# Spreading the gates of two expert pairs at once from two copies of the gate rows

## The reference

```python
# 1: linear attention over 8 heads of 8 channels, on layer-normed channels
k = relu(conv1x1(x, Wk, bk)); q = relu(conv1x1(x, Wq, bq)); v = conv1x1(x, Wv, bv)
context = einsum('bhkn,bhvn->bhkv', k, v)          # over all 16384 positions
x = x + conv1x1(einsum('bhkv,bhkn->bhvn', context, q), Wr, br)
# 2: mixture of 8 experts per position, on layer-normed tokens t
probs = softmax(t @ router_w + router_b); top_p, top_i = top_k(probs, 2)
top_p = top_p / sum(top_p)
expert_out = einsum('bnd,edc->bnec', t, expert_w) + expert_b
t = t + sum over the two chosen experts of top_p * expert_out
```

## Time and profile before

| what | value |
|---|---|
| median of 3 runs | 672.26 us (671.27 to 673.7) |
| the profiled execution | 671.9 us, its span 670.1 us |
| granted TensorE clock, mean | 0.992 |
| PE busy | 616.2 us, 92% |
| DVE, ACT, POOL busy | 515.1 (77%), 425.2 (63%), 396.1 us (59%) |
| spread matmuls, L1078 | 1024, busy 93.2 us |
| expert matmuls, L1092 and L1095 | 512 each, side by side, 243.6 us |
| DMA, mean | 129 GB/s |

### The profile page before, as it was taken

One profiled execution on the slowest core, in us unless ns is written; L12 is line 12 of the kernel. 1 busy time (PEld: TensorE's weight loads), 2 busy tenths in 40 slices (PEclk: granted clock), 3 DMA queues, 4 the chain that ended last, 5 costly groups with the idle time before them and its releaser, 6 DMA issues.

```text
span 670.1 us, 21498 instructions
## 1 busy us (share of the span) xinstructions
PE 616.2 (92%) x8318; PEld 276.3 (41%) x8318; DVE 515.1 (77%) x1176; ACT 425.2 (63%) x832; POOL 396.1 (59%) x350
## 2 busy tenths in 40 slices
PE   3799989779999999999999999999999999998887
PEld 1566656444444444444444444444332332332222
DVE  3534455978888888889788787987799999989844
ACT  2355545576666675766757576766766776766642
POOL 7232342237565655666666556655577777777875
PEclk9799989999999999999999999999999999999999
DMA  6223635666555566655545665554565667446542
GB/s 149 56 76 79 146 97 129 150 167 159 122 122 134 126 147 146 159 142 138 133 111 130 147 152 127 129 116 104 133 154 127 157 172 170 101 111 142 126 111 48
DMA packets 32662, 86.21 MB, mean 129 GB/s; under 512 B 7650, under 2 KB 7826, under 8 KB 32562
## 3 DMA queue, kind: packets, MB, share of 16 engines
q1 hardware_dynamic: 32082, 84.64, 52.8%
q0 software_dynamic: 288, 0.19, 0.2%
q10 hardware_dynamic: 192, 0.01, 0.0%
HBM read 34.47 MB, written 16.78 MB: 76 GB/s over the span
## 4 chain that ended last, share of the span: by engine, by line
PE 62%; DVE 18%; ACT 10%; issue 7%; DMA 1%; POOL 1%; ACTq 0%; DVEq 0%; SPq 0%; POOLq 0%
PE bank L1092 26%; PE bank L1078 7%; PE bank L1015 5%; PE bank L993 4%; PE bank L979 4%; DVE z L826 3%; PE bank L938 3%; PE bank L1089 3%; PE bank L962 3%; DVE x L731 3%; ACT grows L569 2%; DVE xnT L686 2%; PE bank L1039 2%; DVE osb L836 2%; ACT L529 2%
## 5 line engine op out<-in xcount | busy, mean ns | idle before, releaser
L442 POOL TENSOR_TENSOR z<-gbs,x1d 128x512 f32<-128x512 f32 x256 | 320.2, 1275 | 185.2 <-ACT gbs L575 72.6
L1095 PE MATMUL bank<-z,ew 128*64 128x512 f32 x512 | 243.7, 598 | 0.0
L1092 PE MATMUL bank<-z,ew 128*64 128x512 f32 x512 | 243.6, 598 | 0.0
L826 DVE TENSOR_TENSOR z<-bank,x1d 128x512 f32<-128x512 f32 x256 | 164.7, 675 | 16.2 <-PE bank L1078 16.2
L575 ACT COPY gbs<-bank 128x512 f32<-128x512 f32 x256 | 140.7, 594 | 43.8 <-PE bank L1078 41.3
L433 POOL TENSOR_TENSOR xsq<-xin 128x512 f32<-128x512 f32 x64 | 65.4, 1043 | 81.7 <-DMA xin<-in_x_dram 76.0
L1078 PE MATMUL bank<-grows,sel 64*64 64x512 f16 x1024 | 93.2, 387 | 16.3 <-ACT grows L569 7.3
L1092 PEld LDWEIGHTS bank<-z,ew 128*64 128x64 f32 x512 | 64.9, 136 | 104.6 <-issue 96.3
L503 ACT COPY xn<-bank 128x512 f32<-128x512 f32 x64 | 34.4, 589 | 62.8 <-PE bank L938 62.8
L1095 PEld LDWEIGHTS bank<-z,ew 128*64 128x64 f32 x512 | 64.7, 136 | 0.0
L686 DVE TENSOR_TENSOR xnT<-bank,rstd 128x512 f32<-128x512 f32 x64 | 41.0, 682 | 30.2 <-PE bank L924 28.5
(11 more groups left out here) (135 smaller groups left out, 804.8 us busy)
## 6 DMA issues: line engine op xcount, KB each, us to landing
x1d<-x SPq DMA_DIRECT2D x128, 256.0 KB, 4.5
xin<-in_x_dram SPq DMA_DIRECT2D x64, 256.0 KB, 4.2
x_again<-in_x_dram SPq DMA_DIRECT2D x64, 256.0 KB, 4.2
out_dram<-osb SPq DMA_DIRECT2D x128, 128.0 KB, 2.4
k<-in_const_dram SPq DMA_DIRECT2D x1, 453.5 KB, 3.8
ew_nat<-in_L_ffn_expert_w_dram POOLq DMA_DIRECT2D x2, 64.0 KB, 6.4
sel<-in_const_sel_dram SPq DMA_DIRECT2D x1, 128.0 KB, 3.4
bk_rows<-bk_wide ACTq DMA_DIRECT2D x6, 1.0 KB, 1.7
```

The lines of the kernel that those rows point to most:

```text
L442: pool.tensor_tensor(z[:, 1, i % R_Z, :], gbs[:, i % R_Z, :], x1d[:, g % 2, 1, u * NT:(u + 1) * NT], ALU.mult).then_inc(z_pool, 1)
L826: dve.tensor_tensor(z[:, 0, i % R_Z, :], bank[:, :], x1d[:, g % 2, 0, u * NT:(u + 1) * NT], ALU.mult).then_inc(taken_of(("spread", i, 0)), 1)
L1092: pe.matmul(out_bank[0:C, :], ew[:, j, :], z[:, 0, i % R_Z, :], start=False, stop=(j == PAIRS - 1), skip_group_check=True).then_inc(prod_d ...
L1095: pe.matmul(out_bank[C:P, :], ew[:, j, :], z[:, 1, i % R_Z, :], start=False, stop=(j == PAIRS - 1), skip_group_check=True).then_inc(prod_d ...
```

## The change

Three things are done.

1. Each spread of an iteration becomes two matmuls, one for each half, of 32 contraction rows by 128 outputs. The iterations with even `j` read rows 0 to 31 and 64 to 95 of `grows`; those with odd `j` read rows 32 to 63 and 96 to 127 of a new tile, `grows_again`, into which SP copies the 16 gate rows of each half with a transfer (`repeat_gates`, two transfers for each group). `sel` has its ones for kinds 4 and 5 as well. The two iterations of a slot so use four different row tiles of the array, and four banks. PE waits for the transfers before the second iteration of each group; SP waits for `take_gate_rows` before it issues them.
2. In slot 2 both spreads come first, ahead of the queries, on PE, in the list of banks, and with their copies and products on ACT and DVE.
3. On DVE the second part of `x_deviations` stands behind the gate steps of slot 3; on ACT the square of x1 is one instruction of 1024 elements instead of two of 512.

```diff
 def bank_uses():
             if k == 2:
+                for i in iterations(n, k + 1):
+                    yield from (("spread", i, s) for s in range(S))
                 if real(n - L_KEYS):
                     yield from (("queries", n - L_KEYS, s) for s in range(S))
-                for i in iterations(n, k + 1)[:1]:
-                    yield from (("spread", i, s) for s in range(S))
                 if real(n - L_ATTEND):
                     yield from (("attended", n - L_ATTEND, u) for u in range(U))
...
-            for i in iterations(n, k + 1)[1 if k == 2 else 0:]:
+            for i in iterations(n, k + 1) if k != 2 else []:
...
-            sel[hit & (kind == 0), p, m] = 1.0
-            sel[hit & (kind == 1), p, m] = LO
+            sel[hit & (kind % 4 == 0), p, m] = 1.0
+            sel[hit & (kind % 4 == 1), p, m] = LO
...
+        grows_again = sb("grows_again", [P, 2, NP], F16)
...
+            def repeat_gates(g):
+
+                when_taken(sp, ("gate_rows", g, 0))
+                if g == 0:
+                    sp.wait_ge(cleared, 4)
+                if g >= 2:
+                    for s in range(S):
+                        when_taken(sp, ("spread", (g - 1) * U * PAIRS - 1, s))
+                for s in range(S):
+                    sp.dma_start(grows_again[C * s + 32:C * s + 32 + 2 * E, g % 2, :],
+                                 grows[C * s:C * s + 2 * E, g % 2, :]).then_inc(grows_again_in[g % 2], 16)
...
                 if n + 1 >= R_X and real(n + 1):
                     load_x(n + 1)
+                if real(n - L_TURN_GATES):
+                    repeat_gates(n - L_TURN_GATES)
                 if real(n - L_EXPERTS):
                     store(n - L_EXPERTS, 0)
...
-            for tile in (w_nat, rw_nat, eb_in):
+            for tile in (w_nat, rw_nat, eb_in, grows_again):
...
-            def square_x1(g, u):
-                when_taken(act, ("attended", g, u))
+            def square_x1(g):
+                for u in range(U):
+                    when_taken(act, ("attended", g, u))
...
             def take_gate_rows(g):
+                if g >= 2:
+                    act.wait_ge(grows_again_in[g % 2], 32 * (g // 2))
... (DVE, the loop over slots)
                     if k == 2:
                         if real(n - L_EXPERTS):
                             result(n - L_EXPERTS, 0)
-                        for i in iterations(n, k + 1)[:1]:
+                        for i in iterations(n, k + 1):
                             product(i)
                         if real(n - L_ATTEND):
                             for u in range(U):
                                 residual(n - L_ATTEND, u)
-                    if k == 3 and real(n - L_COLS):
-                        x_deviations(n - L_COLS, 4, N_XSTAT)
                     for phase, (k0, k1) in gates_by_phase.items():
                         if quad_in(n, k, phase) is not None:
                             gates(quad_in(n, k, phase), k0, k1)
+                    if k == 3 and real(n - L_COLS):
+                        x_deviations(n - L_COLS, 4, N_XSTAT)
... (PE)
             def broadcast(i):
                 g, u, j = iteration(i)
                 if u == 0 and j == 0:
                     when_taken(pe, ("gate_rows", g, 0))
+                if u == 0 and j == 1:
+                    pe.wait_ge(grows_again_in[g % 2], 32 * (g // 2 + 1))
+                source = grows_again if j % 2 else grows
                 for s in range(S):
-                    use, rows = ("spread", i, s), slice(C * s, C * s + C)
+                    use = ("spread", i, s)
                     bank = when_free(pe, use)
-                    for a in range(2):
-                        cols = slice(C * a, C * a + C)
-                        ins = pe.matmul(bank[cols, :], sel[rows, j, cols], grows[rows, g % 2, u * NT:(u + 1) * NT],
-                                        start=True, stop=True)
-                    ins.then_inc(filled_of(use), 1)
+                    first = C * s + 32 * (j % 2)
+                    pe.matmul(bank[:, :], sel[first:first + 32, j, :],
+                              source[first:first + 32, g % 2, u * NT:(u + 1) * NT], start=True, stop=True
+                              ).then_inc(filled_of(use), 1)
```

More of the change, by code:

```diff
@@ L253, in metaformer_block @@
         x1d_in = [sem(f"x1d_in{i}") for i in range(2)]
+        grows_again_in = [sem(f"grows_again_in{i}") for i in range(2)]
         stored = [sem(f"stored{i}") for i in range(2)]
@@ L529, in root_x @@
                 nc.scalar.activation(xstat[:, 4, :], xstat[:, 3, :], ACT.Sqrt).then_inc(xstat_root, 1)
-            def square_x1(g, u):
-                when_taken(act, ("attended", g, u))
+            def square_x1(g):
+                for u in range(U):
+                    when_taken(act, ("attended", g, u))
                 if g:
                     when_filled(act, ("rows", g - 1 + L_ROUTE, 0))
-                nc.scalar.activation(x1sq[:, u * NT:(u + 1) * NT], x1[:, g % R_X1, u * NT:(u + 1) * NT], ACT.Square
-                                     ).then_inc(x1_squared, 1)
+                nc.scalar.activation(x1sq[:, :], x1[:, g % R_X1, :], ACT.Square).then_inc(x1_squared, 1)
             def root_dev(p):
@@ L619, in _ @@
                     if k == 2:
+                        for i in iterations(n, k + 1):
+                            copy_gates(i)
                         if real(n - L_KEYS):
@@ L622, in _ @@
                                 take_queries(n - L_KEYS, s)
-                        for i in iterations(n, k + 1)[:1]:
-                            copy_gates(i)
-                    for i in iterations(n, k + 1)[1 if k == 2 else 0:]:
+                    for i in iterations(n, k + 1) if k != 2 else []:
                         copy_gates(i)
@@ L632, in _ @@
                         if real(n - L_ATTEND):
-                            for u in range(U):
-                                square_x1(n - L_ATTEND, u)
+                            square_x1(n - L_ATTEND)
                     for phase, step in gate_steps.items():
@@ L1008, in make_rows @@
                 if real(g):
-                    pe.wait_ge(x1_squared, (g + 1) * U)
+                    pe.wait_ge(x1_squared, g + 1)
                     parts += [(x1[:, g % R_X1, :], route_w[:, :]), (x1sq[:, :], route_square_w)]
@@ L1144, in _ @@
                     if k == 2:
+                        for i in iterations(n, k + 1):
+                            broadcast(i)
                         if real(n - L_KEYS):
                             make_queries(n - L_KEYS)
-                        for i in iterations(n, k + 1)[:1]:
-                            broadcast(i)
                         if real(n - L_ATTEND):
```

## The result

The changed kernel takes 773.31 us (median of 4 runs, 771.61 to 777.57), the kernel before on the same chip 672.98 (4 runs). The ratio is 1.150, with a 95% interval of 1.147 to 1.153. The forecast was 727 us, its range 703 to 750: the sign and the wait that it named are there, the size is not; 46 us are missing. The profiled execution took 774.96 us, its span is 773.2 (670.1 before).

A forecast was written before the change was run, and what follows sets the result against it. PE was taken to bound the kernel, its stages standing end to end. Waits of 67.4 us less 12.7 us saved gave net 54.7 on 671.9 us, so 727 us, with a range of 703 to 750.

The forecast's parts named there:

- The wait for the transfer: Slot 3, 16 full steps: PE waits for the transfer, turn to experts 4.53 us in place of 2.98, cost 24.8 us.
- Late steps: Slot 3, other 16 steps: turn to experts 4.53 us against 2.28, four with 0.64 more; cost 27.0 and 9.0 us.
- The product moved ahead: Slot 2's second product ahead of DVE's gate steps: 0.6 us in each of eleven steps, 6.6 us; full steps nothing.
- The spreads: Four matmuls on four row tiles run at once: 0.35 us a spread, 0.21 less; 5.0 us saved in slot 1.
- Slot 0 of heavy steps: Eight heavy full steps: DVE catches up, the spread goes from 0.84 to 0.36 us, 3.8 us saved.
- Slot 2: Light full steps take 2.55 us to the bias matmul, 0.22 less, 2.2 us saved; heavy full steps gain 0.
- Deviations: nothing: On DVE, moving the deviations behind the gate steps costs nothing, as DVE does the same work.
- Hidden transfer: Rival: the wait for the transfer never ends last in slot 3; 652 us, chance 0.07.
- Slow landing: Rival: transfers land as slow as the slowest store, 4.0 us; 794 us, chance 0.07.
- Two row tiles at a time: Rival: the four row tiles run two at a time, 0.21 us more in each of 96 spreads; 747 us, chance 0.10.
- Relief: Rival: added waits let ACT and DVE run ahead, heavy slot 2 and late slots 0 and 2 gain; 711 us, chance 0.16.

The follow-up runs named there:

- f2: The changed kernel with nine more matmuls over all 128 rows of the array ahead of each group's first spread: 740.42 us.
- a2: The changed kernel with slot 2 back in the order of before (queries, spread, attended, spread): 763.66 us.
- d1: The kernel before with only the second part of the deviations moved behind the gate steps of slot 3: 678.33 us.
- a1: The changed kernel, but each group's second iteration reads its own rows of `grows`, so the transfer is needed two iterations later: 705.61 us.
- f1: The changed kernel with nine more matmuls over 32 rows of the array ahead of each group's first spread: 759.39 us.

## Why the prediction was wrong

- **The step that failed is the one that isn't there: what PE's waits do to the matmuls behind them.** The sum took durations from rows at 2.4 GHz for work that would stand behind gaps of up to 3.3 us. The experts of the 32 steps take 258.7 us from start to start after, 230.1 before: 28.6 us, and the bias matmuls beside them 2.0. f2 shows at least 33 of the 46 us missing to be of this kind. The rows to ask gave no warning by themselves: in the earlier trace rows PE waits 1.10 us at a clock of 1.00, and from the first spread on no wait of before is longer than 1.1. But ahead of it the trace of before has both cases: a wait of 3.3 us up to 138.9 with a clock of 1.00 behind it, and a fall to 0.50 around a wait of 1.6 us that ends at 86.0:

```profile
85.80:89.20 3.40, 3.20 (x48) 2.84 (x51) 1.11 (x5) 0.31 (x1) 2.95 (x6) 0.50 0.60 159
```

That should have widened the range upwards.
- **"The wait for the transfer", full steps: chain right, start wrong in most.** Six of 16 come out nearly as worked (4.67, forecast 4.53; the issues are 0.6 apart, not 0.54, and the landing is 1.99, not 1.9). In seven the copy is late too, and in three the second transfer lands 2.7 to 3.3 us behind its issue (in one of these both); turn to experts is 5.1 to 6.6 there. The first step takes 8.3, but it took 6.7 before, where the forecast puts 2.98. All 16 sum to 86.2 us from turn to experts, 51.3 before: 34.9 more, where the forecast has 24.8.
- **Late steps: the sum is right, partly by luck.** Turn to experts sums to 81.9 us over 16; the terms (4.53 each, 0.64 in four, 0.6 in eleven) give 81.6. But the copy is late in nine steps and not in fifteen, and each step is 0.1 to 0.3 longer than 4.53 even where the copy is on time; in one the transfer is slow.
- **"The product moved ahead": "in full steps nothing" was wrong.** The copy's slack was measured against when ACT was free before, though what holds ACT is DVE's gate steps, and those are moved by the product. With the order back (a2) the copy is on time in full steps and the kernel 10 us faster; the forecast has 6.6 for the product and takes off 2.2 for slot 2.
- **"The spreads", slot 1: right**, 0.32 to 0.33 for 0.35. With the loss for four row tiles that the prediction took from the Trainium skill (page "TensorE: Matmul & The Clock Gate", section "Measured speedup vs the span model") 0.42 was the estimate, and the measured length is below it. Whether some of that loss is in the 0.32 stays open, since no run gives the price of changing the shape for this group alone.
- **Slot 0 of heavy steps: relief came**, the spread takes 0.32.
- **Slot 2: wrong in sign.** 3.03 for 2.55 in light steps, since neither the late banks nor the change of shape at the queries was in the sum. In heavy steps about 4.0 for 3.77.
- **"Deviations: nothing": wrong as a price**, 5 us alone (d1), 29 in a1. "DVE does the same work" counted the work and not its neighbour on POOL. What it costs in the changed kernel's own time is open.
- **The rivals.** Hidden transfer: refuted, all 32 waits are there. Slow landing: refuted, 2.0 at the median and 3.3 at most. Two row tiles at a time: refuted by 415.35 and 415.36. Relief: only in slot 0.

Put together, the spans differ by 103.1 us, 102.3 of them from the first turn on. Turn to experts has 77.8 of these (168.0 against 90.2; the forecast's waits are 67.4), the experts 28.6, and all other stages together give back 4.1, where the forecast saves 12.7. What is not settled is what makes the clock fall. In the changed kernel it falls in 21 of the 25 steps with a transfer wait of 1.96 us and over. In four of that size it does not (2.40, 2.24, 2.22 and 2.22, one of them at 401.80), and in a2 it falls behind five waits of 1.52 and 1.53 us.

## What to carry to other kernels

A wait put on the engine that bounds the kernel costs its length, and may cost as much as half again in the matmuls behind it: before pricing it, look whether the trace shows such a wait and what clock stands behind it, and if none does, put that into the range. Ask of every moved instruction on DVE what POOL runs beside it, and of every matmul whose shape is changed what shape its neighbours have: here the neighbours took back what the packed spread saved. If a copy in another place is needed at once, let the first reader use the original: this (a1) was worth 68 us.

## What the runs showed of the hardware

- In the changed kernel PE's granted clock fell to 0.50 in 21 of the 25 steps with a transfer wait of 1.96 to 3.27 us, and in none of the six with 1.54 to 1.55; in a2 it fell behind five of 1.52 and 1.53, in a1 behind 1.49 and 1.48. The Trainium skill (page "TensorE: Matmul & The Clock Gate", section "HAM oscillation — how this bites in real kernels") tells of the same pattern, a wait for a DMA in each turn of a loop and a cold start behind it; the trace agrees, with the numbers above.
- With nine filler matmuls over 128 rows (f2) no stretch at half clock begins between the first spread and PE's last matmul; with nine of the same length over 32 rows (f1) ten do.
- Four matmuls in four row tiles of 32 start within 10 ns and take 0.32 us between other shapes; a stage whose neighbour changes its shape takes about 0.1 us longer. The Trainium skill (page "TensorEngine Tiling (Array Packing)", section "Key Properties") says that a change of tiling mode drains TensorE, and gives no time; the rows agree and give one.
- Inside SBUF 32 KB land 1.9 to 2.1 us behind the issue in most groups and 3.3 at most, and two transfers in a row on one queue are 0.6 us apart.
- Two-input DVE steps of 0.17 us last 1.2 us when they start under a POOL product, and end within 37 ns of its end (30 of them in a1).
